# Values of layer 0 in blocks of 128 context rows, dealt to their sequences by stores cut at multiples of 16 rows

## What is computed

```
x = x + tanh(g_xattn[0]) * L0_xattn(layernorm(x), ctx)    # 8 heads of 64
x = x + tanh(g_ffn[0])   * L0_ffn(layernorm(x))           # 8 experts, the best 2 for a token
x = x + tanh(g_xattn[1]) * L1_xattn(layernorm(x), ctx, ctx)
x = x + tanh(g_ffn[1])   * L1_ffn(layernorm(x))

# in L0_xattn
q = x @ Wq;  k = ctx @ Wk;  v = ctx @ Wv
attn = softmax(q @ k.T * 64 ** -0.5)                      # for each head
return (attn @ v) @ Wo + bo
```

## Time and profile before

| | us |
|---|---|
| median of three runs | 786.98 (784.69 to 788.65) |
| the profiled run | 788.87 |
| its span | 787.1 |
| busy in the span: PE / DVE / ACT / POOL | 672.4 / 574.3 / 448.7 / 475.7 |
| mean granted clock of TensorE | 0.928 of full speed |
| attention of layer 0, first to last score product | 33.78 to 245.16 |

### The profile page before, as it was taken

One profiled execution on the slowest core, in us unless ns is written; L12 is line 12 of the kernel. 1 busy time (PEld: TensorE's weight loads), 2 busy tenths in 40 slices (PEclk: granted clock), 3 DMA queues, 4 the chain that ended last, 5 costly groups with the idle time before them and its releaser, 6 DMA issues.

```text
span 787.1 us, 17248 instructions
## 1 busy us (share of the span) xinstructions
PE 672.4 (85%) x4720; PEld 609.5 (77%) x4720; DVE 574.3 (73%) x2005; ACT 448.7 (57%) x1219; POOL 475.7 (60%) x693
## 2 busy tenths in 40 slices
PE   6888988988887889988979898899888886878896
PEld 5667887877776889987878787788887886877796
DVE  3467877788667587999896888988878753845772
ACT  3466755665454555766666776676576543434451
POOL 4035346667457777787463344676566567677771
PEclk9999989998789799999998999999899986999998
DMA  9637546434344234545633534433534013344645
GB/s 263 176 82 191 161 136 172 120 112 128 102 113 131 86 102 115 151 117 143 174 87 90 118 90 90 129 100 76 119 93 99 24 43 96 107 120 122 188 132 178
DMA packets 130990, 95.91 MB, mean 122 GB/s; under 512 B 30504, under 2 KB 119112, under 8 KB 130832
## 3 DMA queue, kind: packets, MB, share of 16 engines
q1 hardware_dynamic: 113200, 69.15, 33.5%
q0 software_dynamic: 9088, 19.68, 7.7%
q10 hardware_dynamic: 8608, 5.99, 2.7%
HBM read 55.09 MB, written 44.10 MB: 126 GB/s over the span
## 4 chain that ended last, share of the span: by engine, by line
PE 40%; DVE 26%; issue 10%; ACT 9%; DMA 6%; POOL 5%; SPq 1%; DVEq 1%; ACTq 0%; POOLq 0%
PE banks L1032 9%; PE banks L896 4%; PE banks L1051 4%; DVE row_max L1265 4%; DMA y_rows<-y_sb,result_at 3%; DVE prob L1268 3%; PE banks L776 3%; PE banks L881 2%; PE banks L778 2%; PE banks L777 2%; PE banks L840 2%; POOL x_rows L1687 2%; ACT vo L1156 2%; POOL y_rows L1694 2%; PE banks L863 2%
## 5 line engine op out<-in xcount | busy, mean ns | idle before, releaser
L1694 POOL DMA_INDIRECT y_rows<-y_sb,result_at x156 | 151.0, 968 | 57.0 <-issue 30.2
L1032 PE MATMUL banks<-xb,up 128*128 128x128 f32 x936 | 143.5, 293 | 15.9 <-DVE hidden L1513 5.0
L1687 POOL DMA_INDIRECT x_rows<-xm,row x128 | 127.6, 997 | 36.0 <-issue 30.2
L1032 PEld LDWEIGHTS banks<-xb,up 128*128 128x128 f32 x936 | 125.9, 204 | 22.3 <-issue 10.1
L1051 PE MATMUL banks<-down,hidden 128*128 x624 | 100.4, 285 | 9.3 <-DVE y_sb L1530 8.7
L1649 POOL TENSOR_TENSOR v_flat<-v_raw,row_head 104x64 f32<-104x64 f32 (+1 forms) x128 | 55.7, 464 | 74.3 <-ACT v_raw L1187 73.9
L1051 PEld LDWEIGHTS banks<-down,hidden 128*128 128x128 f32 x624 | 85.5, 198 | 12.5 <-issue 12.1
L896 PE MATMUL banks<-v_flat,prob_t 128*128 128x108 f32 (+2 forms) x640 | 88.7, 288 | 3.2 <-issue 1.6
L896 PEld LDWEIGHTS banks<-v_flat,prob_t 128*128 128x128 f32 (+1 forms) x640 | 81.9, 202 | 11.0 <-ACT prob_t L1171 6.2
L1265 DVE TENSOR_REDUCE row_max<-banks 128x8 f32<-128x616 f32 x96 | 75.6, 787 | 20.4 <-PE banks L840 11.9
L1171 ACT ACTIVATE prob_t<-banks 128x512 f32<-128x512 f32 x192 | 72.6, 432 | 28.1 <-PE banks L863 26.2
(11 more groups left out here) (212 smaller groups left out, 1619.8 us busy)
## 6 DMA issues: line engine op xcount, KB each, us to landing
v_rows<-vo SPq DMA_DIRECT2D x64, 154.0 KB
vo_flat<-v_rows SPq DMA_DIRECT2D x32, 256.0 KB
x_norm<-x_rows SPq DMA_DIRECT2D x86, 72.0 KB
x_far<-x_rows SPq DMA_DIRECT2D x70, 72.0 KB
gathered<-y_rows ACTq DMA_DIRECT2D x32, 128.0 KB
q_rows<-up_raw SPq DMA_DIRECT2D x8, 512.0 KB, 2.8
q_even<-q_rows SPq DMA_DIRECT2D x12, 256.0 KB
q_odd<-q_rows SPq DMA_DIRECT2D x12, 256.0 KB
```

Source lines behind the costliest of these rows:

```text
L1032: done = pe.matmul(banks[:, UP_BANK[i % 2], part * P:(part + 1) * P], block_w[:, i % WR, part // 2, part % 2 * P:(part % 2 + 1) * P], xb[: ...
L1687: pool.indirect_dma_start(out=x_rows[i // HG][:, :], out_offset=bass.IndirectOffsetOnAxis(ap=row[:, n, c:c + 1], axis=0), in_=xm[:, i % 2, ...
L1694: pool.indirect_dma_start(out=y_rows[k][:, :], out_offset=bass.IndirectOffsetOnAxis(ap=result_at[:, i % (2 * YR):i % (2 * YR) + 1], axis=0 ...
```

## The change

The values are made by blocks of 128 flat context rows: task `("v0", n, h)` is now half h of block n, 20 x 2 units of 128 rows (32 in the last block) instead of 32 x 2 of 77. A block holds rows of two or three sequences. Each sequence has its own part of `v_rows`, and `value_pieces` deals a block's rows to them: each sequence's share is a store of a multiple of 16 rows, and what is left over is a store of its own. That gives 94 pieces for a half, 188 stores. `value_halves` spreads the units over the steps: as many as the next sequence's load needs, and otherwise 5 in 4 steps. The first unit of a step stands in the first place, others in the second.

```diff
+DMA_ROWS = 16
+def value_halves():
+    begun, out = 2, []
+    for u in range(NSEQ):
+        last = ((min(u + 2, NSEQ) * NKEY) - 1) // P
+        n = min(max(2 * (last + 1), (5 * (u + 1) + 13) // 4), 2 * CTX_BLOCKS)
+        out.append([("v0", k // 2, k % 2) for k in range(begun, n)])
+        begun = n
+    return out
...
-            step += [("v0_load", u)] + [("v0", u + 1, 0)][:u + 1 < NSEQ] + [("divide0", u)] + more[1]
+            step += [("v0_load", u)] + values[u][:1] + [("divide0", u)] + more[1]
...
-            step += [("v0", u + 1, 1)][:u + 1 < NSEQ] + [("bias0", u)] + more[2]
+            step += values[u][1:] + [("bias0", u)] + more[2]
...
-    v_rows = [nc.dram_tensor(f"v_rows{i}", [UNIT_ROWS, D], F32, kind="Internal").ap() for i in (0, 1)]
+    v_rows = nc.dram_tensor("v_rows", [NSEQ, UNIT_ROWS, D], F32, kind="Internal").ap()
...
+        def value_pieces(n):
+            rows = range(n * P, min((n + 1) * P, CTX_ROWS))
+            out = []
+            for r in [r for r in rows if r == rows[0] or r % NKEY == 0]:
+                count = min(NKEY - r % NKEY, rows[-1] + 1 - r)
+                even = count - count % DMA_ROWS
+                out += [(r // NKEY, r % NKEY, r - n * P, even)] if even else []
+                out += [(r // NKEY, r % NKEY + even, r - n * P + even, count - even)] if count > even else []
+            return out
...
-                    half_rows = v_rows[b % 2][h * (UNIT_ROWS // 2):(h + 1) * (UNIT_ROWS // 2), :]
-                    w.wait_ge("v0", 2 * b + h + 1)
-                    w.wait_ge(f"v0_in{b % 2}", 32 * (b // 2))
-                    sync.dma_start(half_rows.rearrange("(a n) d -> n a d", n=NKEY), vo0[:, h, :, :]).then_inc(sem("v0_out"), 16)
+                    n, h = t[1:]
+                    w.wait_ge("v0", 2 * n + h + 1)
+                    for b, key, first, count in value_pieces(n):
+                        to = v_rows[b].rearrange("(a n) d -> n a d", n=NKEY)[key:key + count, 4 * h:4 * h + 4, :]
+                        sync.dma_start(to, vo0[first:first + count, h, :, :]).then_inc(sem(f"v0_out{h}"), 16)
+                        values_out[h] += 16
                 elif t[0] == "v0_load":
...
-                    w.wait_ge("v0_out", 32 * (b + 1))
+                    for h in (0, 1):
+                        w.wait_ge(f"v0_out{h}", values_out[h])
...
-                    done = three_pass(banks[0:NKEY, V_BANK, :], ctx_th[:, c0:c0 + NKEY], ctx_tl[:, c0:c0 + NKEY], four(wvo_h), four(wvo_l))
+                    done = three_pass(banks[0:cols.stop - cols.start, V_BANK, :], ctx_th[:, cols], ctx_tl[:, cols], four(wvo_h), four(wvo_l))
...
-                    w.wait_ge("v0_out", 32 * b)
+                    w.wait_ge(f"v0_out{h}", 16 * sum(len(value_pieces(m)) for m in range(n)))
```

## The result

The changed kernel took 774.06 us (median of 4 runs, 773.12 to 775.61) against 785.84 for the kernel before on the same chip, a ratio of 0.985 with a 95% interval of 0.982 to 0.988. That is 11.8 us less, where the prediction said 25. The direction held and the time lies in the range, but less than half of the forecast came.

What follows compares the result with a forecast made beforehand. TensorE was taken as the nearest bound of layer 0's attention, VectorE close behind. Columns 18.7 and waits 13.4 us, less about 7 given back by VectorE, made -25 us from 787.0: 762 us, range 745 to 779.

Steps and rivals of the forecast that it cites:

- (a): Layer 0 attention: 40 value units for 64 take 18.7 us off TensorE; ScalarE's 14.1 us of fewer copies count nothing.
- (b): Layer 0 attention: TensorE's 25.2 us of waits for value evictions shrink, net 13.4 us, 8.8 staying in six heavy steps.
- (c): Layer 0 attention: VectorE's unchanged work becomes the longer one in some steps, so about 7 us come back.
- (d): TensorE's granted clock in layer 0 attention: bounds 0 and -15 us, taken as 0.
- (e): SyncE's 188 stores for 64 add 35 us of issue at 284 ns each, covered by early loads: taken as 0.
- The rival of SyncE's loop: Stores, their landing and loads set each step of layer 0 attention: 21 us more than now, 808; chance 0.05.
- the signs named in advance: Profile if right: 120 products, stage near 186 us, VectorE 85%, eviction waits under 5 us, waits for VectorE up to 9.

Runs made afterwards that it cites:

- e4_after_samecols: The changed kernel with the three products made twice in 24 of its 40 value units: ratio 0.992 to the kernel before, stage 199.04 us.
- e4_before_fewcols: The kernel before with one product of 128 columns in 24 of 64 value units, waits kept: ratio 0.991, stage 204.51 us.
- f3_nocols: The changed kernel with each of its 40 value units cut to one product of 128 columns: ratio 0.983 to the kernel before, stage 197.60 us.
- e6_heavy: The changed kernel with 12 for 13 in the spreading formula, moving seven second value units into heavy steps: ratio 0.994 to the kernel before.
- e7_after_keys: The changed kernel with a step's second key group moved ahead of the exponential: 774.60 us, ratio 0.985 to the kernel before.
- e2_uncut: The changed kernel with pieces not cut at multiples of 16 rows, 102 stores instead of 188: 822.92 us, ratio 1.045 to the kernel before.
- e1_pieces: The changed kernel with value loads reading the input context, all 188 stores kept: 777.80 us, ratio 0.988 to the kernel before.
- e1_one: The changed kernel with value loads reading the input context and one store per unit, 40 for 188: 769.78 us, ratio 0.976 to the kernel before.
- f5b_copies: The changed kernel with an unused 128x512 ScalarE copy added from step 3 on where the second value place is empty: ratio 0.989 to the kernel before.
- g1_fewer: The changed kernel with pieces left whole where their rows have a divisor from 10 to 16, 136 stores: 830.57 us against 845.06 before, ratio 0.985.

## Why the prediction was off

By its own steps, with what the runs put in their place (us of the stage, steps 7 and 8 left out where nothing else is said):

| step | predicted | measured, stage |
|---|---|---|
| (a) 24 units of columns | 18.7 | 3.5 to 4.5 (e4_after_samecols against after), 7.1 (e4_before_fewcols against before) |
| (a) ScalarE's 24 fewer copies | 0 | 3.8 to 4.7 for 9.6 us of copies (some 6 to 7 for 14.1, in proportion) |
| (b) waits for the eviction, net | 13.4 | 16.6 with the copies in it (samecols against before); some 10 without them |
| (c) VectorE gives back | -7 | not a term: 24.8 us less of its work gives 3 to 5 |
| (d) clock of the stage | 0 | 0.92 to 0.94, and 0.92 in the second profile |
| (e) stores | 0 | -1 to -4, in steps 7 and 8, which were left out above |
| sum | 25 | 18.4 (17.3 for the two second profiles) |

The rows do not add up exactly: what the columns return depends on whether the waits are gone.

**The step that failed is the first half of (a)**: "TensorE loses 24 x 0.78 = 18.7 us, counted at the full clock", taken off the stage's length. The number of products and their pitch were right; that they lie on the path in every step was not. In light steps they do (0.7 of 0.78 for a unit), in the heavy ones they hardly do, and all together returned 4 to 7 us. The unit is also missing once in 22 steps and twice in step 30, not once in 24. Two things kept the rest. The one is the clock: the granted clock of 0.62 behind a wait was read as a loss that could only get smaller, and f3_nocols shows that it can grow: less work, a clock of 0.87, and 8.9 us less busy for some 28 us of products. The other is that TensorE's 28.7 us of idle were already there; removing work in a step whose length another chain sets only adds to it, as the 5.88 and 5.90 us of step 13 show.

**The second is in (b)**, "TensorE will run on only to the next thing that VectorE owes it: the low part of a key, 107.98", taken for all six heavy steps. In the step that I read, step 11, it is right: the bank that the rank products need is freed by the first key unit, whose low part ends at 107.98. Steps 11 and 19 together gained 3.1 to 3.6 us (15.9 and 16.2 before, 12.6 and 12.7 after) where 3.4 were counted. But in steps 15 and 23 the bank is held by the second key unit, and there the eviction's wait stood in front of a later one. In step 15 before, the value unit that waited, the second low part and the rank products were:

```profile
138.06 0.45 PE L776 MATMUL banks<-wvo_h,ctx_th 128*77 128x512 f32 x1 [1.96 <-ACT vo L1156]
...
138.51 0.43 DVE L1281 TENSOR_TENSOR k_t<-banks,k_t 128x308 fp32r<-128x308 f32 x1
...
139.09 0.25 PE L996 MATMUL banks<-picked,earlier 128*128 128x32 f32 x1
```

The low part ends at 138.94, and the rank products start 0.15 us later, behind the value unit. In step 15 of after they start 0.14 us behind the low part, so without wait and unit there was nothing to gain here. After the change the wait shows as itself, 3.07 us in step 15 (the row of 132.84 above). In the six heavy steps 11.0 us of waits for low parts stand where 14.2 for evictions did; 8.8 were foreseen. Their length fell by 8 us (53.2 and 53.0 to 45.1), but in 15 and 23 by 0 to 0.6, and in the router steps 13 and 21, which have the same second key unit, by nothing. For these four steps the sum had 3.1 us of columns and 1.8 of waits, and 0 to 0.6 came. e6_heavy and the move of the keys in e7_after_keys bear the reading out from two sides.

**(c) named the wrong thing.** I expected a second engine's total to take over. The totals say little here: 28 us of TensorE's products, 24.8 of VectorE's reductions and 9.6 of ScalarE's copies moved the stage of after (without steps 7 and 8) by +1 to +2, -4 to -5 and +4 to +5 us. Per us of work ScalarE's copies were the dearest, though it is the idlest of the three. The copies that were added, and those that the change removed, stand at the end of ScalarE's step, behind the turned probabilities; step 12 above shows one way by which they reach a key's low part, and whether it is the main one was not tested.

**ScalarE "is not a bound and I count nothing for it"** was the same error with the other sign, and it covered part of the miss.

**(e)** priced an issue at 284 ns; it was 406 in the median and about 0.46 in a row of six, so SyncE's step was longer than 3.0 us where table loads stood in it as well, and at step 7 the cover (a load is used two steps after its issue) was gone: the load issued at 75.83, in step 7, is the one that step 7 uses. ScalarE's waits for stores, counted as gone, were 6.1 us in 4 in place of 3.9 in 3. The rival of SyncE's loop setting every step did not come; e2_uncut shows its mechanism, when landings and not issues are long. The 8.0 us between the medians of e1_pieces and e1_one stay without a place.

Right were the 120 products, TensorE's wait for evictions under 5 us (3.8), and the rest of the program, within the spread of its profiles though not within 2 us. Of the signs named in advance the stage (193 for 186), VectorE's share (81% for 85%) and TensorE's waits for VectorE (18 us for k_t alone, where 9 were named) missed, and it is the last that carries the cause. That the time fell inside the stated range is in part luck: the columns term was three to five times too large, and the 7 us of (c), which VectorE did not take, and the copies made up for part of it.

What stays open: how the 16.6 us of waits and copies divide, since f5b_copies adds copies of 0.46 us in place of 0.59 and its ratio alone does not tell them from nothing; whether steps 13, 15, 21 and 23 would gain if the keys took the banks in the other turn there, or the router and rank products had a bank of their own, neither of which was tried; and whether g1_fewer is truly 2 to 3 us faster than after. No version with the right output was shown to beat the kernel after.

## What to carry to other kernels

A removed piece of work is worth its time only if it lies on the loop that sets the step. Write that loop down from the timeline, from one recurring instruction to its next, with every engine's part and no gap; work beside it counts at little however full its engine is, and work in it counts. Do it for each kind of step: where a resource goes round in turn (here two banks), two steps that look the same in the timeline can wait for different instructions, and the kernel's own bookkeeping says for which. When a wait is to go, look for the instruction that would be waited for next among those that end after the wait too, not only before it: a later one is invisible as long as the first stands in front of it.

## What the runs showed of the hardware

When products were taken from TensorE, its granted clock fell: some 28 us of products fewer, 0.94 (0.92 in a second profile) to 0.87 over the stage, and only 8.9 us less busy time. With 24 units doubled it was 0.96. Each of the two changed kernels has one profile.

Small stores are not cheap to issue in a row: 284 ns when a step had two, 406 in the median of 188, and 2.77 us for six. Where the pieces were left whole, 47, 53, 71 and 73 rows among them, stores landed far later: evictions stood up to 9.3 us for them, and the whole kernel became 4.5% slower than before, with fewer stores (102) than the version that was faster (188).

Chips differ in one stage and not in another: 211.4 and 211.8 us for the attention stage of before on two chips, and 541.9 and 608.7 us for all behind it.
